# One core of a Perceiver block: stacked keys for the scores, two of three down blocks of the experts in split passes, and a new order in two passages

## The chip, the cores and the metric

The kernel is one program on one core of a Trainium2 chip. The metric is the time of one execution in device microseconds (us). Before the change it is 1679.32 us, the median of 3 runs (1677.81 to 1680.35).

## The reference, cut to what matters

A stream `x` of 512 rows (8 batches of 64 latents, width 512) passes six residual blocks in float32: causal cross attention to the first 64 context rows, self attention with tied queries and keys, a mixture of experts, masked cross attention to all 1601 context rows, causal self attention, and an int8 product. The change touches the third and the fourth, and the passage into each.

```python
# mixture of experts: 512 tokens, 64 experts, 8 per token; I = 352; two shared halves of the same size
rw = _route(x, gate_w, gate_bias)                       # [512, 64], 8 non-zero weights in a row
expert_out = silu(x @ Wg[e].T) * (x @ Wu[e].T) @ Wd[e].T
out = sum_e rw[:, e] * expert_out[e] + shared(x)        # shared = _mlp(x, Sg, Su, Sd)

# cross attention: 16 heads of 32, 8 batches, 64 queries, 1601 keys
attn = softmax(where(mask, -inf, einsum('bhqd,bhkd->bhqk', Q, K) * scale))
out = einsum('bhqk,bhkd->bhqd', attn, V) @ Wo + bo
```

## The kernel before, in words

Every engine has its own instruction list, written out by hand; semaphores join them. Nothing reorders an engine's list, so its order is the order of calls in the functions named here. PS is the PSUM, 8 banks of 512 floats.

**Float32 products in two ways.** A float32 matmul costs TensorE (PE) several internal passes; the trace counts two instructions for each. The large products are split instead: an operand is rounded to fp32r (`_hi`), the rest is `_lo`, and three fp32r passes hi*hi + hi*lo + lo*hi take its place (`gate_up` line 2144, `group` line 1267). ScalarE (ACT) makes the hi part by a copy, VectorE (DVE) the lo part by a subtraction; for the context GpSimd (POOL) makes the lo part.

**Shared experts and routing** (line 739 on). Per half tile k of 8: gate and up matmuls (`shared_in`), ACT's silu, DVE's product, three transposes of it, two ACT copies of these (`shared_ht`), and three float32 matmuls with the down weights (`shared_out`, which holds the transposes too, so PE waits between its two halves for the copies). Between them stand the matmuls of the routing tables (`table`), for which DVE works at the same time.

**Expert loop** (line 2130 on). 64 tiles of 128 token slots, four buffers k; tile i = 4r + k. On PE a step of tile i is: gate of i (12 matmuls), transposes of the hidden rows of i-1 (`hidden_t`), transposes of the gathered rows of i+1 (`rows_t`), up of i (12), down of i-1 (`down`: blocks of 128, 128 and 96 hidden rows, float32). ACT: silu, `rows_high`, `weights_high` of tile i+2, the weighted output `rows_out_copy`, and the issue of the two down-weight loads. DVE: `hidden_copy`, `rows_low`, `mul`, `weights_low`. SyncE (SP) loads the gate and up weights, POOL gathers the rows of a tile and scatters its output with add into HBM, each after a small copy of the slot numbers (lines 2085, 2100).

**Passage into the cross attention** (lines 1386 and 1576 on). PE makes 2 of the first batch's key chunks and 12 value tiles (`PRE[0]`), while the expert sums come back from HBM and are normalised; then it turns the rows (`xt_pe`), makes all four query blocks (`q_pe`), and the first scores with what is left of keys and value tiles (`PRE[1]`).

**Cross attention** (SEQ, line 1159). 32 units (batch b, dc); a unit handles four heads, and its list interleaves `k` (key chunk, 12 matmuls), `v` (value tile, 12), `s` (scores of a chunk), `T` (transposes of the probabilities of this unit), `P` (probabilities times values), `z` (divisors). The scores made in a unit are those of the next one. A chunk of keys (384, 384, 384 and 450 wide) has 128 feature rows: rows 0-63 belong to head pair p = 0, rows 64-127 to p = 1. `score` (line 1311) multiplies each half with the same half of the queries, 64 rows deep, three passes for each p, six matmuls in all. ACT writes a chunk's hi part (`key_high`), DVE its lo part (`key_low`), POOL the two parts of the queries (`take_q`).

## Time and profile before

| | |
|---|---|
| median of 3 runs | 1679.32 us |
| profiled execution | 1682.47 us, span 1680.6 us, mean granted TensorE clock 0.993 |
| front, first two attentions | 0 to 130 us |
| shared experts and routing | 130 to 214 us |
| expert loop | 214 to 679 us |
| passage into the cross attention | 679 to 740 us |
| cross attention, 8 batches | 740 to 1558 us |
| last attention and int8 block | 1558 to 1680.6 us |
| PE busy, over the span | 1634.1 us (97%) |
| DVE, ACT, POOL busy | 58%, 38%, 27% |

The bounds of the stages are read off the chain that ended last. In that chain PE holds 93% of the span. Its largest lines are L1305 (values, 18%), L1296 (keys, 17%), L2157 (gate and up, 14%), L2180 (down, 9%), L1323 (scores, 6%) and L1343 (transposes, 6%).

### The profile page before, as it was taken

To read this page: it belongs to the slowest core of one execution; us is meant where nothing else is said; L and a number is where in the kernel's file an instruction comes from. 1 tells how busy PE (TensorE), PEld (TensorE's weight loads), DVE (VectorE), ACT (ScalarE), POOL (GpSimd) and SP (SyncE) were. 2 spreads that over 40 slices of the span, in tenths; PEclk is the share of its full clock that TensorE was granted. 3 is DMA by queue.
4 is the path that set the end of the run, shared out by engine and by line. 5 is a ranking of instruction groups with operands and counts; after the bars stand their busy time and mean duration, and the time that the engine had idled before them with its cause. 6 is when DMAs were issued, how large, how long until landed. Compare 5 with 4: busy or idle time off the path is not lost.

```text
span 1680.6 us, 35189 instructions
## 1 busy us (share of the span) xinstructions
PE 1634.1 (97%) x13780; PEld 1351.0 (80%) x13781; DVE 966.9 (58%) x2076; ACT 637.0 (38%) x845; POOL 446.1 (27%) x453
## 2 busy tenths in 40 slices
PE   8999999999999999899999999999999999999897
PEld 5666677788777887778998989989899899898583
DVE  3877566667766666545444445454444544544666
ACT  1232156555655555223334233342242332423112
POOL 3110245555555554210302103021030210400100
PEclk9999999999999999999999999999999999999998
DMA  8003399999999998201102001020020200201200
GB/s 302 13 3 118 136 343 335 344 334 337 336 341 336 340 328 286 92 1 40 41 6 80 6 18 64 7 80 6 1 80 6 67 19 2 79 2 35 98 26 27
DMA packets 68476, 214.92 MB, mean 128 GB/s; under 512 B 13106, under 2 KB 30770, under 8 KB 58496
## 3 DMA queue, kind: packets, MB, share of 16 engines
q1 hardware_dynamic: 38656, 153.03, 25.3%
q10 hardware_dynamic: 15360, 43.26, 7.5%
q0 software_dynamic: 14336, 16.83, 4.8%
q8 instruction: 95, 1.56, 0.4%
q14 instruction: 29, 0.24, 0.0%
HBM read 208.07 MB, written 21.76 MB: 137 GB/s over the span
## 4 chain that ended last, share of the span: by engine, by line
PE 93%; DVE 2%; ACT 1%; DMA 1%; issue 1%; SPq 0%; POOL 0%; DVEq 0%; POOLq 0%; ACTq 0%
PE PS L1305 18%; PE PS L1296 17%; PE PS L2157 14%; PE PS L2180 9%; PE PS L1323 6%; PE PS L1343 6%; PE PS L1362 3%; PE PS L390 3%; PE PS L448 2%; PE PS L746 2%; PE PS L2141 2%; PE PS L411 1%; PE PS L762 1%; PE PS L2169 1%; PE PS L1698 1%
## 5 line engine op out<-in xcount | busy, mean ns | idle before, releaser
L1305 PE MATMUL PS<-S_r 128*128 128x256 f32 x2496 | 329.3, 286 | 1.9 <-DVE kh0l L1478 1.9
L1305 PEld LDWEIGHTS PS<-S_r 128*128 128x128 f32 x2496 | 305.0, 189 | 26.6 <-issue 22.2
L1296 PE MATMUL PS<-S_r 128*128 128x384 f32 (+1 forms) x1536 | 307.3, 349 | 0.0
L2157 PE MATMUL PS<-S_r,R_r 128*128 128x352 f32 x1152 | 298.8, 350 | 1.7 <-DVE R_r L2296 1.7
L1296 PEld LDWEIGHTS PS<-S_r 128*128 128x128 f32 x1536 | 266.2, 188 | 10.7 <-DVE kh0l L1478 2.0
L2157 PEld LDWEIGHTS PS<-S_r,R_r 128*128 128x128 f32 x1152 | 199.6, 189 | 20.5 <-issue 18.6
L1431 ACT COPY S<-PS 128x512 f32<-128x512 f32 (+1 forms) x128 | 64.4, 503 | 276.9 <-PE PS L1343 276.9
L1236 POOL COPY S<-qbd 128x128 f32<-128x128 f32 x32 | 9.4, 293 | 536.6 <-PE PS L1323 525.2
L1489 DVE CUSTOM_DVE_ANT_0 R<-PS,maskadd 128x384 f32<-128x384 f32 (+1 forms) x256 | 136.1, 569 | 17.9 <-PE PS L1323 17.9
L1471 DVE TENSOR_TENSOR R<-PS,vbias 128x256 f32<-128x256 f32 (+1 forms) x208 | 88.1, 424 | 101.3 <-PE PS L1305 96.6
L1219 POOL TENSOR_TENSOR S_r<-S,S_r 128x1536 fp32r<-128x1536 f32 (+2 forms) x31 | 114.0, 3686 | 119.7 <-ACT S_r L1408 119.6
L1425 ACT ACTIVATE R<-R,nmx 128x1601 f32<-128x1601 f32 x64 | 104.0, 1629 | 82.9 <-DVE nmx L1497 82.9
L2180 PE MATMUL PS<-R 128*128 128x512 f32 (+1 forms) x288 | 131.7, 593 | 1.3 <-DVE R L2306 1.3
L1478 DVE SCALAR_TENSOR_TENSOR kh0l<-PS,bias_c,kh0h 128x384 fp32r<-128x384 f32 x64 | 39.5, 618 | 141.6 <-ACT kh0h L1415 141.6
L2104 POOL DMA_INDIRECT moe_acc<-x,scol x64 | 102.4, 1600 | 57.1 <-PE PS L2141 36.1
L2019 DVE TENSOR_TENSOR R_r<-R,S_r 128x1408 fp32r<-128x1408 f32 x64 | 101.1, 1622 | 27.0 <-ACT S_r L2011 27.0
L1343 PE MATMUL PS<-ident,R 128*128 128x128 f32 (+1 forms) x832 | 114.1, 275 | 0.8 <-ACT R L1425 0.8
L1478 DVE SCALAR_TENSOR_TENSOR kh1l<-PS,bias_c,kh1h 128x384 fp32r<-128x384 f32 x64 | 41.7, 651 | 115.1 <-ACT kh1h L1415 115.1
L1523 DVE COPY S<-PS 128x512 f32<-128x512 f32 (+1 forms) x128 | 75.0, 586 | 53.8 <-PE PS L1343 53.4
L1343 PEld LDWEIGHTS PS<-ident,R 128*128 128x128 f32 (+1 forms) x832 | 93.7, 140 | 8.2 <-issue 3.0
L2011 ACT CAST S_r<-R 128x1408 fp32r<-128x1408 f32 x64 | 84.3, 1365 | 41.7 <-PE PS L2157 41.7
L2100 POOL COPY scol<-idx_tab 128x1 int32 (+1 forms) x64 | 62.2, 971 | 111.9 <-ACT x L2238 109.1
(261 smaller groups left out, 2462.6 us busy)
## 6 DMA issues: line engine op xcount, KB each, us to landing
R<-in_w_gu SPq DMA_DIRECT2D x34, 1408.0 KB, 9.7
R<-in_w_dna ACTq DMA_DIRECT2D x45, 512.0 KB, 5.5
qbd<-in_w_gu SPq DMA_DIRECT2D x16, 1408.0 KB, 9.4
S<-in_w_gu SPq DMA_DIRECT2D x16, 1408.0 KB, 9.5
S<-in_ctxT SPq DMA_DIRECT2D x24, 768.0 KB, 4.7
...
```

The lines of the kernel that those rows point to most:

```text
L1219: nc.gpsimd.tensor_tensor(lo, raw, hi.bitcast(F32), ALU.subtract).then_inc(s, 1)
L1296: last = nc.tensor.matmul(PS[:, bank, 0:n], w3[0][:, cc, f0:f0 + P], x3[i][:, cc, 0:n], start=(cc == 0 and w3 is wkv_hi and x3 is ctx_hi), ...
L1305: last = nc.tensor.matmul(PS[:, bank, 0:256], x3[need][:, cc, k0:k0 + P], w3[1][:, cc, f0:f0 + 256], start=(cc == 0 and w3 is wkv_hi and x ...
L1323: last = nc.tensor.matmul(PS[:, p, 0:n], q3[r:r + 64, :], k3[r:r + 64, 0:n], start=(q3 is qh and k3 is kh_), stop=(q3 is ql))
L1343: last = nc.tensor.transpose(PS[0:n, 2 + p, i * P:(i + 1) * P], sx[2 * (dc % 2) + p][:, kt * P:kt * P + n], ident[:, :])
L1425: nc.scalar.activation(v, v, ACT.Exp, scale=SC, bias=nmx[:, p:p + 1], accum_out=rsx[:, p:p + 1]).then_inc(px_ready, 1)
L1471: nc.vector.tensor_tensor(vx[hf][0:n, i, :], PS[0:n, bank_of(b, dc, ("v", i)), 0:256], vbias[0:n, hf * 256:hf * 256 + 256], ALU.add).then_ ...
L1489: nc.vector.tensor_tensor_reduce(out=sx[2 * ((dc + 1) % 2) + p][:, k0:k0 + n], in0=PS[:, p, 0:n], in1=maskadd[:, k0:k0 + n], scale=1.0, sc ...
L2019: nc.vector.tensor_tensor(wgu_lo[k][:, c, :, :], wgu[k][:, c, :, :], wgu_hi[k % 2][:, c, :, :].bitcast(F32), ALU.subtract).then_inc(wl_rea ...
L2104: pool.indirect_dma_start(out=acc[k % 2], out_offset=bass.IndirectOffsetOnAxis(ap=scol[:, k:k + 1], axis=0), in_=yrow[k], in_offset=None, ...
L2157: last = nc.tensor.matmul(PS[:, gu, 0:I], x3[:, c, :], w3[:, c, gu, :], start=(c == 0 and x3 is hi[0] and w3 is hi[1]), stop=(c == NC - 1 ...
L2180: last = nc.tensor.matmul(PS[:, 3, :], hT[0:w, j, :], wdn[k][0:w, j, :], start=(j == 0), stop=(j == 2))
```

## The change

The program does these things differently:

- **Scores.** For each p the keys are stacked: hi part in the 64 rows of p, lo part in the other 64. The queries of p stand twice, in both halves, once as hi and once as lo part. Two matmuls over all 128 rows per p, four a chunk, give (hi + lo)(hi + lo). `key_high`, `key_low` run once per p on 64 rows, DVE's output going to the other 64; `take_q` makes four small copies and two operations of twice the width.
- **Down blocks.** Blocks 0 and 1 of `down` become three fp32r passes each (`hT_hi`, `hT_lo`, `wdn_hi`, `wdn_lo`), block 2 stays float32 and comes first. ACT makes `hT_hi`, copies block 2 and makes `wdn_hi`; DVE makes `hT_lo` and `wdn_lo`.
- **Loads.** The down weights are loaded by SP behind the gate and up weights, no longer by ACT.
- **Slot numbers.** DVE copies a tile's two columns (`columns`); POOL's two small copies go.
- **Shared experts.** `shared_in` is called for gate and up apart, and the transposes are a piece of their own (`shared_turned`); the pieces are spread, and the last `shared_out` stands behind `rows_t(0, 0)`.
- **Passage.** `PRE` and DVE's list are reordered: `v0` ahead of `k0`, the four masks later, the query blocks among the first scores.

The diff, cut to its core (line indents are shortened):

```diff
...
-qraw, qzero = (R1[:, 2 * NC * SP + i * P:2 * NC * SP + (i + 1) * P] for i in range(2))
-kh = [[sb(f"kh{i}{half}", [P, KN[3]], F32R) for half in "hl"] for i in range(2)]
-qb = [[sb(f"qb{i}{half}", [P, P], F32R) for half in "hl"] for i in range(2)]
+qraw, qzero = (R1[:, 2 * NC * SP + 2 * i * P:2 * NC * SP + 2 * (i + 1) * P].rearrange("p (a m) -> p a m", a=2)
+               for i in range(2))
+kq = sb("kq", [P, 4 * KN[3] + 8 * P], F32R)
+keys = [[kq[:, (2 * i + p) * KN[3]:(2 * i + p + 1) * KN[3]] for p in range(2)] for i in range(2)]
+qb = [[kq[:, 4 * KN[3] + (4 * i + 2 * half) * P:4 * KN[3] + (4 * i + 2 * half + 2) * P]
+       .rearrange("p (a m) -> p a m", a=2) for half in range(2)] for i in range(2)]
+m = Arena(kq[:, :])
+wdn_hi = [m.view(2, D) for _ in range(2)]
+hT_lo = m.view(2, P)
...
+    def shared_turned(k):
+        hf = k % 2
         pe.wait_ge(sh_h, k + 1)
         if k >= 1:
             pe.wait_ge(sh_ht, k)
...
+    def shared_out(k):
+        t, hf = k // 2, k % 2
         pe.wait_ge(sh_ht, k + 1)
...
-PRE = ["k0 v0 v1 v2 k1 v3 v4 v5 v6 v7 v8 v9 v10 v11", "s0 k2 s1 k3 v12 s2 s3"]
+PRE = ["v0 k0 v1 v2 k1 v3 v4 v5 v6 v7 v8 v9 v10 v11", "q0 q1 s0 q2 k2 s1 k3 s2 v12 s3 q3"]
...
-        nc.gpsimd.tensor_copy(qraw[:, :].unsqueeze(1) if not isinstance(bv, int) else qraw[:, :],
-                              qbd[:, dc, bv, :]).then_inc(q_taken, 1)
-        pool.wait_ge(q_taken, 4 * b + dc + 1)
-        nc.gpsimd.tensor_tensor(hi[:, :], qraw[:, :], qzero[:, :], ALU.add).then_inc(qh_set, 1)
+        for i in range(4):
+            p, half = i // 2, i % 2
+            nc.gpsimd.tensor_copy(qraw[64 * half:64 * half + 64, p, :],
+                                  qbd[64 * p:64 * p + 64, dc, bv, :]).then_inc(q_taken, 1)
+            pool.wait_ge(q_taken, 4 * (4 * b + dc) + i + 1)
+        nc.gpsimd.tensor_tensor(hi[:, :, :], qraw[:, :, :], qzero[:, :, :], ALU.add).then_inc(qh_set, 1)
         pool.wait_ge(qh_set, 4 * b + dc + 1)
-        nc.gpsimd.tensor_tensor(lo[:, :], qraw[:, :], hi[:, :].bitcast(F32),
+        nc.gpsimd.tensor_tensor(lo[:, :, :], qraw[:, :, :], hi[:, :, :].bitcast(F32),
                                 ALU.subtract).then_inc(ql_ready, 1)
...
-        pe.wait_ge(kl_ready, 4 * h + c + 1)
-        if not (isinstance(b, int) and b < 0 and c == 0):
-            pe.wait_ge(sx_read, 8 * h + 2 * c)
-        (qh, ql), (kh_, kl_) = qb[(dc + 1) % 2], kh[c % 2]
-        for q3, k3 in ((qh, kh_), (qh, kl_), (ql, kh_)):
-            for p in range(2):
-                r = 64 * p
-                last = nc.tensor.matmul(PS[:, p, 0:n], q3[r:r + 64, :], k3[r:r + 64, 0:n],
-                                        start=(q3 is qh and k3 is kh_), stop=(q3 is ql))
-                if q3 is ql:
-                    last.then_inc(sx_made, 1)
+        for p in range(2):
+            pe.wait_ge(kl_ready, 8 * h + 2 * c + p + 1)
+            if h or c:
+                pe.wait_ge(sx_read, 8 * h + 2 * c + p - 1)
+            for half in range(2):
+                last = nc.tensor.matmul(PS[:, p, 0:n], qb[(dc + 1) % 2][half][:, p, :], keys[c % 2][p][:, 0:n],
+                                        start=(half == 0), stop=(half == 1))
+            last.then_inc(sx_made, 1)
...
-        nc.scalar.activation(kh[c % 2][0][:, 0:n], PS[:, bank_of(b, dc, ("k", c)), 0:n], ACT.Identity,
-                             bias=bias_c[:, 3, f:f + 1]).then_inc(kh_ready, 1)
+        for p in range(2):
+            r = slice(64 * p, 64 * p + 64)
+            nc.scalar.activation(keys[c % 2][p][r, 0:n], PS[r, bank_of(b, dc, ("k", c)), 0:n], ACT.Identity,
+                                 bias=bias_c[r, 3, f:f + 1]).then_inc(kh_ready, 1)
...
-        hi, lo = kh[c % 2]
-        dve.wait_ge(kh_ready, 4 * key_half(b, dc) + c + 1)
-        nc.vector.scalar_tensor_tensor(out=lo[:, 0:n], in0=PS[:, bank_of(b, dc, ("k", c)), 0:n],
-                                       scalar=bias_c[:, 3, f:f + 1], in1=hi[:, 0:n].bitcast(F32),
-                                       op0=ALU.add, op1=ALU.subtract).then_inc(kl_ready, 1)
+        for p in range(2):
+            r, other = slice(64 * p, 64 * p + 64), slice(64 - 64 * p, 128 - 64 * p)
+            k = keys[c % 2][p]
+            dve.wait_ge(kh_ready, 8 * key_half(b, dc) + 2 * c + p + 1)
+            nc.vector.scalar_tensor_tensor(out=k[other, 0:n], in0=PS[r, bank_of(b, dc, ("k", c)), 0:n],
+                                           scalar=bias_c[r, 3, f:f + 1], in1=k[r, 0:n].bitcast(F32),
+                                           op0=ALU.add, op1=ALU.subtract).then_inc(kl_ready, 1)
...
-    made(("k", 0), ("v", 0), ("v", 1))
+    made(("v", 0))
     first_rest(2, 0)
+    made(("k", 0), ("v", 1))
...
-    made(("v", 4))
-    set_mask(0, 0)
-    set_mask(0, 1)
-    made(("v", 5))
-    set_mask(0, 2)
-    set_mask(0, 3)
-    made(("v", 6))
...
-    made(("v", 10))
     for t in range(NT):
         last = nc.vector.bn_aggr(mv[:, t, :], st[:, t, :])
     link(last)
     nc.vector.tensor_scalar(rstd[:, :], mv[:, :, 1], EPS, None, ALU.add).then_inc(mv_ready, 1)
+    made(("v", 10))
+    set_mask(0, 0)
     dve.wait_ge(rstd_ready, MV[3] + 1)
     scaled(0)
...
-    q_dve(dve, 2, 2, bank=2)
+    set_mask(0, 1)
+    set_mask(0, 2)
+    set_mask(0, 3)
     for w in PRE[1]:
...
+        def load_dn(r, k):
+            i = NBUF * r + k
+            ev = expert(r, k)
+            if not (isinstance(r, int) and r == 0):
+                sp.wait_ge(y_made, i - NBUF + 1)
...
-        with sp.Fori(1, n) as r:
+        for k in range(NBUF):
+            load_gu(1, k)
+            if k:
+                load_dn(1, k - 1)
+        with sp.Fori(2, n) as r:
             for k in range(NBUF):
-                load(r, k)
+                load_gu(r, k)
+                load_dn(*tile_before(r, k))
+        load_dn(n - 1, NBUF - 1)
...
-            pool.wait_ge(tables, 1)
+            col_set, turned = (count(pool, v) for v in (i + 1, i - NBUF + 1))
             pool.wait_ge(rows_out, 32)
             if not (isinstance(r, int) and r == 0):
-                pool.wait_ge(xg_made, i - NBUF + 1)
-            nc.gpsimd.tensor_copy(gcol[:, k:k + 1], idx_tab[:, column(r, k)]).then_inc(gcol_set, 1)
-            col_set = count(pool, i + 1)
-            pool.wait_ge(tables, 1)
-            pool.wait_ge(gcol_set, col_set)
+                pool.wait_ge(xg_made, turned)
+            pool.wait_ge(cols_set, col_set)
...
+        for i in range(2):
+            rest(wkv_lo[i], slot[1 + 2 * i], wkv_hi[i], w_lo, w_hi, i + 1)
         n = iterations(pool)
         for k in range(NBUF):
             gather(0, k)
...
-            for j, (i0, w) in enumerate(IJ):
-                last = nc.tensor.matmul(PS[:, 3, :], hT[0:w, j, :], wdn[k][0:w, j, :],
-                                        start=(j == 0), stop=(j == 2))
+            nc.tensor.matmul(PS[:, 3, :], hT[0:IJ[2][1], 2, :], wdn[k][0:IJ[2][1], 2, :], start=True, stop=False)
+            pe.wait_ge(dl_ready, i + 1)
+            for j in range(2):
+                for h3, w3 in ((hT_hi, wdn_hi[k % 2]), (hT_lo, wdn_hi[k % 2]), (hT_hi, wdn_lo[k])):
+                    last = nc.tensor.matmul(PS[:, 3, :], h3[:, j, :], w3[:, j, :],
+                                            start=False, stop=(j == 1 and w3 is wdn_lo[k]))
             last.then_inc(y_made, 1)
...
         rows_t(0, 0)
+        shared_out(2 * NT - 1)
...
-        def load_down(r, k):
-            e = act.value_load(eot_row[0:1, column(r, k)], min_val=0, max_val=E - 1)
...
+        def hidden_high(r, k):
+            i = NBUF * r + k
+            act.wait_ge(ht_made, i + 1)
+            if not (isinstance(i, int) and i == 0):
+                act.wait_ge(y_made, i)
+            nc.scalar.copy(hT[0:96, 2, :], PS[0:96, 2, 2 * P:3 * P])
+            nc.scalar.copy(hT_hi, PS[:, 2, 0:2 * P].rearrange("p (a b) -> p a b", a=2)).then_inc(hh_ready, 1)
+        def down_high(r, k):
+            i = NBUF * r + k
+            act.wait_ge(w_dn[k], 32 * (r + 1))
+            if not (isinstance(r, int) and r == 0 and k < 2):
+                act.wait_ge(y_made, i - 1)
+            nc.scalar.copy(wdn_hi[k % 2], wdn[k][:, 0:2, :]).then_inc(dh_ready, 1)
...
+            if not (isinstance(r, int) and r == 0 and k == 0):
+                hidden_high(*tile_before(r, k))
             if not (final and k == NBUF - 1):
                 rows_high(*tile_after(r, k))
+            down_high(r, k)
             if not (final and k >= NBUF - 2):
                 weights_high(*tile_after(*tile_after(r, k)))
             if not (isinstance(r, int) and r == 0 and k == 0):
                 rows_out_copy(*tile_before(r, k))
-                if not (final and k):
-                    load_down(*(tile_before(r + 1, k) if k else (r, NBUF - 1)))
...
+        hidden_high(n - 1, NBUF - 2)
+        down_high(n - 1, NBUF - 1)
         act.wait_ge(u_made, NBUF * n - 1)
         ctx_high(0, 0)
         act.wait_ge(u_made, NBUF * n)
         ctx_high(0, 1)
+        hidden_high(n - 1, NBUF - 1)
...
-        def hidden_copy(r, k):
+        def hidden_low(r, k):
             i = NBUF * r + k
-            dve.wait_ge(ht_made, i + 1)
+            dve.wait_ge(hh_ready, i + 1)
             if not (isinstance(i, int) and i == 0):
                 dve.wait_ge(y_made, i)
-            nc.vector.tensor_copy(hT[:, 0:2, :], PS[:, 2, 0:2 * P].rearrange("p (a b) -> p a b", a=2))
-            nc.vector.tensor_copy(hT[0:96, 2, :], PS[0:96, 2, 2 * P:3 * P]).then_inc(ht_ready, 1)
-        first_dve(dve)
+            nc.vector.tensor_tensor(hT_lo, PS[:, 2, 0:2 * P].rearrange("p (a b) -> p a b", a=2),
+                                    hT_hi.bitcast(F32), ALU.subtract).then_inc(ht_ready, 1)
+        def down_low(r, k):
+            dve.wait_ge(dh_ready, NBUF * r + k + 1)
+            nc.vector.tensor_tensor(wdn_lo[k], wdn[k][:, 0:2, :], wdn_hi[k % 2].bitcast(F32),
+                                    ALU.subtract).then_inc(dl_ready, 1)
...
+        def columns(r, k, final):
+            dve.wait_ge(xg_loaded[k], 16 * r)
...
+                last = nc.vector.tensor_copy(cols[:, k, :], pairs[:, k, at])
+            last.then_inc(cols_set, 1)
...
+            columns(r + 1, k, final)
             mul(r, k)
+            down_low(r, k)
             if not (final and k >= NBUF - 2):
                 weights_low(*tile_after(*tile_after(r, k)))
...
```

The three places of which the prediction speaks. First PE in the shared experts. `R,xnT` are gate or up matmuls, `ident,R` the transposes of the hidden rows, `R 128x512` the down matmuls, `S` those of the routing. Before:

```order
L746 MATMUL PS<-R,xnT 128x352 x16
L756 MATMUL PS<-ident,R 128x128 x2
L756 MATMUL PS<-ident,R 96x128
L762 MATMUL PS<-R 128x512 x3
L746 MATMUL PS<-R,xnT 128x352 x8
L756 MATMUL PS<-ident,R 128x128 x2
L756 MATMUL PS<-ident,R 96x128
L762 MATMUL PS<-R 128x512 x3
L784 MATMUL PS<-S 128x64 x10
L787 MATMUL PS<-S 128x64 x4
L746 MATMUL PS<-R,xnT 128x352 x8
```

After:

```order
L753 MATMUL PS<-R,xnT 128x352 x16
L763 MATMUL PS<-ident,R 128x128 x2
L763 MATMUL PS<-ident,R 96x128
L753 MATMUL PS<-R,xnT 128x352 x4
L772 MATMUL PS<-R 128x512 x3
L753 MATMUL PS<-R,xnT 128x352 x4
L763 MATMUL PS<-ident,R 128x128 x2
L763 MATMUL PS<-ident,R 96x128
L798 MATMUL PS<-S 128x64 x10
L801 MATMUL PS<-S 128x64 x4
L772 MATMUL PS<-R 128x512 x3
L753 MATMUL PS<-R,xnT 128x352 x8
```

Between a half tile's transposes and its down matmuls there now stand four matmuls of another, or routing.

Second ACT in the expert loop, one tile: `R<-PS 128x352` is the silu, `R_r<-PS 128x512` `rows_high`, the two 1408-wide casts `weights_high`, `x<-PS,w_tab` the weighted output. Before:

```order
L2227 ACTIVATE R<-PS 128x352 [waits h_ready,g_made]
L2220 CAST R_r<-PS 128x512 [waits u_made,xg_made]
L2011 CAST S_r<-qbd 128x1408 [waits u_made,w_gu0]
L2011 CAST S_r<-qbd 128x1408
L2238 ACTIVATE x<-PS,w_tab 128x512 [waits y_made]
L2242 TENSOR_LOAD eot_row
L2242 ISA x2
L2244 ISA
L2244 DMA xnT<-in_w_dna 128x1024
L2246 ISA
L2246 DMA xnT<-in_w_dnb 96x512
```

After:

```order
L2278 ACTIVATE R<-PS 128x352 [waits h_ready,g_made]
L2297 COPY R<-PS 96x128 [waits y_made,ht_made]
L2298 CAST R_r<-PS 128x256
L2268 REGISTER_ALU
L2271 CAST R_r<-PS 128x512 [waits u_made,xg_made]
L2306 CAST kq<-xnT 128x1024 [waits y_made,w_dn1]
L2049 CAST S_r<-R 128x1408 [waits u_made,w_gu3]
L2049 CAST S_r<-R 128x1408
L2288 ISA [waits y_made]
L2289 ISA [waits y_added0]
L2289 ACTIVATE x<-PS,w_tab 128x512
```

The three copies of the hidden rows and of the down weights (`kq`) are new, and the loads are gone.

Third PE at the start of the cross attention. `kh..,qb..` (before) and `kq` (after) are scores, `xnT,R` query blocks, `S_r 128x384` and `128x450` key chunks, `S_r 128x256` value tiles. Before:

```order
L348 MATMUL PS<-ident,S 128x128 x16
L369 MATMUL PS<-xnT,R 128x512 x16
L1323 MATMUL PS<-kh0h,qb0h 128x384 x2
L1323 MATMUL PS<-kh0l,qb0h 128x384 x2
L1323 MATMUL PS<-kh0h,qb0l 128x384 x2
L1296 MATMUL PS<-S_r 128x384 x12
L1323 MATMUL PS<-kh1h,qb0h 128x384 x2
L1323 MATMUL PS<-kh1l,qb0h 128x384 x2
L1323 MATMUL PS<-kh1h,qb0l 128x384 x2
L1296 MATMUL PS<-S_r 128x450 x12
L1305 MATMUL PS<-S_r 128x256 x12
```

After:

```order
L359 MATMUL PS<-ident,S 128x128 x16
L379 MATMUL PS<-xnT,R 128x512 x8
L1355 MATMUL PS<-kq 128x384 x4
L379 MATMUL PS<-xnT,R 128x512 x4
L1330 MATMUL PS<-S_r 128x384 x12
L1355 MATMUL PS<-kq 128x384 x4
L1330 MATMUL PS<-S_r 128x450 x12
L1355 MATMUL PS<-kq 128x384 x4
L1339 MATMUL PS<-S_r 128x256 x12
L1355 MATMUL PS<-kq 128x450 x4
L379 MATMUL PS<-xnT,R 128x512 x4
L1339 MATMUL PS<-S_r 128x256 x12
```

Six half-deep matmuls a chunk (three rows of two) become four full ones, and the query blocks stand apart.

## Rows read from the trace of the kernel before

**Rows 1.** Windows: us; busy us (instructions) of each engine; clock; DMA share; GB/s.

```profile
430.00:437.20 7.20, 7.20 (x39) 5.74 (x39) 5.05 (x7) 4.43 (x6) 3.85 (x4) 1.00 1.01 334
900.00:1007.20 107.20, 106.97 (x1131) 96.68 (x1130) 51.79 (x159) 36.07 (x53) 19.29 (x16) 1.00 0.11 34
```

**Rows 2.** Chain that ended last, expert loop: start us, us, what.

```profile
657.07 1.92 PE PS L2157 x12
658.99 2.58 PE PS L2180 x6
...
666.20 2.58 PE PS L2180 x6
```

**Rows 3.** Groups by line and form: busy us, mean ns, idle before.

```profile
L2011 ACT CAST S_r<-R 128x1408 fp32r<-128x1408 f32 x64 | 84.3, 1365 | 41.7 <-PE PS L2157 41.7
...
L2227 ACT ACTIVATE R<-PS 128x352 f32<-128x352 f32 x64 | 29.7, 464 | 80.8 <-PE PS L2157 74.0 <-issue 6.9
```

**Rows 4.** Timeline of DVE and ACT, routing: start us, us, instruction.

```profile
139.78 0.37 ACT L813 COPY R<-PS 128x256 f32<-128x256 f32 x1 [2.23 <-PE PS L756]
140.05 0.26 ACT L814 COPY R<-PS 96x128 f32<-96x128 f32 x1
...
169.65 1.22 DVE L1119 TENSOR_TENSOR S<-S 128x1024 f32<-128x1024 f32 x1
```

**Rows 5.** Windows of the first loads, as Rows 1.

```profile
2.00:4.00 2.00, 0.00 (x0) 0.00 (x0) 0.00 (x0) 0.00 (x0) 1.26 (x10) 1.00 0.94 299
...
10.00:12.00 2.00, 2.00 (x6) 0.82 (x5) 0.00 (x0) 0.00 (x0) 0.00 (x0) 1.00 1.04 431
```

**Rows 6.** Timeline of the expert loop: a gather and its wait.

```profile
501.10 2.24 POOL L2089 DMA_INDIRECT S<-moe_rows,gcol  x1 [0.83 <-POOL gcol L2085]
...
512.38 0.66 PE L2141 MATMUL PS<-ident,S 128*128 128x128 f32 x4 [1.07 <-DMA S<-moe_rows,gcol]
```

**Rows 7.** Chain that ended last, cross attention.

```profile
812.11 1.42 PE PS L1305 x12
...
814.40 2.09 PE PS L1296 x12
816.49 0.72 PE PS L1323 x6
817.21 3.04 PE PS L1305 x24
...
830.61 2.50 PE PS L1296 x12
...
838.50 0.81 PE PS L1323 x6
```

**Rows 8.** Timeline of PE's weight loads at a score.

```profile
742.48 0.19 PEld L1323 LDWEIGHTS PS<-kh0h,qb1h 64*128 64x128 f32 x2 [0.25 <-issue]
```

**Rows 9.** Timeline, first scores of a unit with dc = 2.

```profile
899.28 0.56 ACT L1415 ACTIVATE kh0h<-PS,bias_c 128x384 fp32r<-128x384 f32 x1
...
899.87 0.62 DVE L1478 SCALAR_TENSOR_TENSOR kh0l<-PS,bias_c,kh0h 128x384 fp32r<-128x384 f32 x1 [3.21 <-ACT kh0h L1415]
```

**Rows 10.** Chain that ended last, shared experts to first expert.

```profile
139.42 0.34 PE PS L756 x3
...
140.37 2.85 PE PS L762 x6
...
211.86 0.56 DVE x L1019
...
213.22 0.70 DVE R_r L2296
```

**Rows 11.** Timeline and chain, passage into the cross attention.

```profile
684.88 4.63 PE L1305 MATMUL PS<-S_r 128*128 128x256 f32 x24 [1.94 <-DVE kh0l L1478]
...
710.13 13.97 PE PS L369 x32
...
736.41 3.35 ACT R L1425 x4
```

More of the change, by code:

```diff
@@ L66, in perceiver @@
         x = sb("x", [P, NT, D])
-        xnT = sb("xnT", [P, NC, T])
+        with nc.sbuf_tensor("xnT", [P, NC, T], F32) as xnT:
+            pass
+        xnT_r = sb("xnT_r", [P, NC, T], F32R)
         with nc.sbuf_tensor("qbd", [P, NC, B, P], F32) as qbd:
@@ L737, in first_pe, with shared_in @@
             logits(3)
-            def shared_in(k):
+            def shared_in(k, gu):
                 t, hf = k // 2, k % 2
                 if k >= 2:
-                    pe.wait_ge(sh_silu, k - 1)
-                    pe.wait_ge(sh_h, k - 1)
-                for gu in range(2):
-                    for c in range(NC):
-                        last = nc.tensor.matmul(PS[:, 2 + 2 * hf + gu, 0:I], xnT[:, c, t * P:(t + 1) * P],
-                                                wgu[2 + hf][:, c, gu, :], start=(c == 0), stop=(c == NC - 1))
-                    last.then_inc(sh_u if gu else sh_g, 1)
-            def shared_out(k):
-                t, hf = k // 2, k % 2
+                    pe.wait_ge(sh_h if gu else sh_silu, k - 1)
+                for c in range(NC):
+                    last = nc.tensor.matmul(PS[:, 2 + 2 * hf + gu, 0:I], xnT[:, c, t * P:(t + 1) * P],
+                                            wgu[2 + hf][:, c, gu, :], start=(c == 0), stop=(c == NC - 1))
+                last.then_inc(sh_u if gu else sh_g, 1)
+            def shared_turned(k):
+                hf = k % 2
                 pe.wait_ge(sh_h, k + 1)
@@ L774, in first_pe @@
             pe.wait_ge(ld_sh, 96)
-            shared_in(0)
-            shared_in(1)
+            shared_in(0, 0)
+            shared_in(0, 1)
+            shared_in(1, 0)
+            shared_in(1, 1)
+            shared_turned(0)
+            shared_in(2, 0)
             shared_out(0)
-            shared_in(2)
-            shared_out(1)
+            shared_in(2, 1)
+            shared_turned(1)
             pe.wait_ge(sel_ready, 1)
@@ L2037, in load @@
                                  a["w_gu2"][ev, :, :].rearrange("e p n -> (e p) n")).then_inc(w_gu[k], 16)
-                    if not isinstance(r, int):
-                        return
-                    if k == 1:
+                def load_dn(r, k):
+                    i = NBUF * r + k
+                    ev = expert(r, k)
+                    if not (isinstance(r, int) and r == 0):
+                        sp.wait_ge(y_made, i - NBUF + 1)
+                    elif k == 1:
                         sp.wait_ge(sh_u, 2 * NT)
@@ L2051, in _ @@
                 for k in range(NBUF):
-                    load(0, k)
+                    load_gu(0, k)
+                    load_dn(0, k)
                     if k == NBUF - 1:
@@ L2112, in _ @@
                     gather(0, k)
-                for i in range(2):
-                    rest(wkv_lo[i], slot[1 + 2 * i], wkv_hi[i], w_lo, w_hi, i + 1)
                 for k in range(NBUF):
@@ L2194, in step @@
                         down(*before)
-                first_pe(pe)
+                shared_out = first_pe(pe)
                 n = iterations(pe)
@@ L2264, in _ @@
                 weights_high(0, 1)
-                for r in range(2):
-                    for k in range(NBUF):
-                        step(r, k)
-                with act.Fori(2, n - 1) as r:
+                for k in range(NBUF):
+                    step(0, k)
+                with act.Fori(1, n - 1) as r:
                     for k in range(NBUF):
```

128 lines of the change are left out of this document (76 added, 52 removed).

## The prediction, made before the changed kernel was run

> **What bounds the kernel now.** I read the page first: TensorE (PE) is busy 97% of the span and holds 93% of the chain that ended last. Then the windows, one expert tile and one batch of the cross attention [rows 1]: PE is busy 7.20 of 7.20 us and 106.97 of 107.20, the next engine (DVE) 5.05 and 51.79. The reader is to see that a saving counts only if it shortens PE's own list, and that ACT (4.43 and 36.07) and DVE have room for more work. Last the chain of waits at the two passages [rows 10, 11], where PE does stop. All sums are made in the profiled execution, 1682.5 us; the median of before is 3.2 us lower, and that is taken off at the end.
>
> **Down blocks, 64 tiles.** Six PE records of a tile's `down` take 2.58 us, 0.43 each [rows 2]. Four of them (blocks 0 and 1) become six fp32r passes of 512 columns. The trace has such passes at other widths: 256 wide 1.42/12 = 0.118, 384 wide 2.09/12 = 0.174, 450 wide 2.50/12 = 0.208 [rows 7], 352 wide 1.92/12 = 0.16 [rows 2]. The line through the first two gives 0.230 at 512. Bounds: 0.16, if width cost nothing, and 0.43, the float32 record. I take 0.23, since four widths lie near one line. So 4 x 0.43 = 1.72 becomes 6 x 0.23 = 1.38, 0.34 less; a tile goes from 7.20 to 6.86, and 64 tiles give 21.8 us. The ends would be +48 and -55.
>
> That holds only if nobody else needs more than 6.86. ACT: 4.43 [rows 1], the two copies of hidden rows 0.37 + 0.26 [rows 4], and the 1024-wide copy of weights, which is not in the trace: between 0.46 at 352 columns and 1.37 at 1408 [rows 3] the line gives 1.04. Sum 6.1. DVE: 5.05 + 1.22 for the 1024-wide subtraction, as the one in the routing [rows 4]; the hidden subtraction takes the place of the old copies; 6.3 at most. Both fit, with 0.5 to 0.8 us to spare. The copies stand ahead of work that PE wants soon: behind `hidden_high` on ACT is `rows_high`, needed by the next gate. Between the transposes and the passes PE has the gathered rows, up (1.92) and block 2 (0.86), which is their cover. Data: 334 GB/s over 7.20 us [rows 1] is 2.40 MB a tile; in 6.86 us that is 351 GB/s. The first loads show 431 for one stretch and 299 for another [rows 5].
>
> POOL loses two small copies before each gather and scatter. One gather kept PE waiting 1.07 us [rows 6]; that its margin grows could give back about 1 us, that the clock of the loads now rests on one queue could take as much. I count nothing.
>
> **End of the expert loop.** On ACT a 1.5 us context copy now stands ahead of the hidden copy of the last tile, and DVE and the last passes are queued behind that. Block 2 covers part of it. Cost 1.0; bounds 0 and 2.
>
> **Shared experts and routing.** From the transposes of a half tile at 139.42 to the end of its down matmuls at 140.37 + 2.85 = 143.22 are 3.80 us [rows 10]. Without the stop it is 0.34 + 2.58 = 2.92, so the stop costs 0.88: two copies, and matmuls that start slower behind it. The chain shows eight such stops; work of another half tile, or routing, now stands in each: 8 x 0.87 = 7.0. The last one is followed by the sum, then two wait steps, and the first expert's gate begins after 213.92 (first row of that stretch at 211.86) [rows 10], 2.1 us; `rows_t(0, 0)` now stands ahead of the last `shared_out`, so they lie beside it. New waits: where a table's matmuls move ahead PE reaches DVE's selection earlier, about 0.6, and the first two tiles' extra copies, 0.5. Sum 8.0; bounds 4 and 10. For the first tiles' loads, which now queue behind gate and up weights, and for a fuller PE in the first stretch I add 0.5, bounds -2 and +2.
>
> **Passage into the cross attention.** PE waits 1.94 us for the first keys' lo part [rows 11]; with `v0` (1.42) ahead of `k0`, 1.4 of it is covered. That alone would buy nothing, since PE waits again later, for DVE to normalise the rows. But DVE's sums start behind the sixth value tile that PE has made, so they come 1.4 earlier too, and one value copy of DVE (0.4) moves behind them: 1.8 in all, counted once. The masks leave a place where DVE waits for PE anyway, nothing. The query blocks took 13.97 in one piece, 3.49 each [rows 11]. Now the first score waits for POOL after two of them: four copies and two double-width operations, some 3 us, with one block (q1) as cover: 1.5 lost at most beyond what it costs now. At the end the fourth block and a value tile stand where PE waited 3.35 us for the exponentials [rows 11]; 3.1 of that goes. Sum 1.8 + 3.1 - 1.5 = 3.4; bounds 0 and 7.
>
> **Scores, 32 units.** A chunk of 384 takes 0.72 [rows 7]: 3 x 0.174 for three pairs of half-deep matmuls that run together, and 0.2 ahead of them. The timeline of weight loads shows the same idle piece, 0.25 at a score's start [rows 8]. Behind a chunk there is one more: 24 value matmuls take 3.04, where twice 1.42 is 2.84 [rows 7], 0.20. So a chunk costs 0.92. Between two full-depth kinds no such piece is in the chain (value tile 812.11 + 1.42, then transposes, then keys at 814.40). Four full matmuls: 4 x 0.174 = 0.70, 0.22 less; the 450-wide chunk 0.81 + 0.20 against 4 x 0.208 = 0.83, 0.18 less. Two p: a unit handles four chunks, 3 x 0.22 + 0.18 = 0.84, times 32 = 27. Of that I take off 0.5: at units with dc = 2 PE reaches the first score while ACT and DVE still write its keys [rows 9], and that takes one step of 0.6 more, eight times, mostly made up by the later ones. 26.5. Bounds: -24 (below) and +27. ACT and DVE get some 2.3 and 2.5 us a unit of 26.8; they have 17 and 13 idle.
>
> [...]
>
> **Sum.** 8.0 + 0.5 + 21.8 - 1.0 + 3.4 + 26.5 = 59.2; 1682.5 - 59.2 - 3.2 = 1620.1, say 1620.
>
> **Rivals.**
> - A, the loop does not get shorter: the data rate or the ACT chain holds the tile at 7.20. For: a mean rate of 334 GB/s of which 351 is asked, DMA share 1.00 or more already [rows 1], ACT only 0.7 us from full, and a gather that has already made PE wait [rows 6]. Against: 431 GB/s for a stretch [rows 5], and PE never idles for weights now. Then 21.8 is missing: 1642. Chance 0.17.
> - B, the 0.4 us around scores belong to something other than half depth, a wait or a change of source, and stay: a chunk takes 0.2 + 0.70 + 0.20 = 1.10, 0.18 more than now; 128 chunks lose 24 instead of gaining 26.5: 1620 + 50 = 1670. Against: [rows 8] name no releaser, only the engine's own issue, and no other neighbours show it. Chance 0.09.
> - C, slower than before: with all weights on one queue, each load behind the one before it, the rate falls to the 299 GB/s of the first stretch [rows 5] or less, since the down weights no longer overlap the gate and up weights. Every microsecond a tile costs 64. The other terms give 37.4, so the point is 7.20 + 37.4/64 = 7.78 us a tile, 309 GB/s; at 288 GB/s a tile takes 8.35 and the time is 1620 + 64 x 1.49 = 1715. Against: in [rows 5] the same single queue reached 431. Chance 0.05.
> - D, the change does not do what it says in the passages: the moved pieces expose as much as they hide, 8.0 + 3.4 go: 1631. Chance 0.08.
>
> **How the numbers follow.** The forecast has 0.58, with a range of its own from 1609 to 1632 (the terms' bounds, not all at one end). 0.03 is for less than that range: passes at 0.21 and a gather margin that gives back more. Between A and C nothing lies near 1679. A measurement of this kernel can tell 0.2%, 3.4 us, from no change. Faster: forecast, the better end, A, B and D, less what B and A together could undo (1692 at worst): 0.93. Same 0.02, slower 0.05. The range 1606 to 1648 holds the forecast, the better end nearly whole, D and A.
>
> **What would show it.** A tile's window of 6.86 with PE busy throughout: right; PE idle with a DMA or `dh_ready` behind it: A or C. Passes of 512 columns at 0.23. Scores at 0.70 a chunk with no issue gap on either side; a gap there is B. In the chain, no stops of ACT copies between 139 and 209, and no 3.35 at 736. Wrong would be a tile above 7.0, or chunks at 0.9 or more.

## The result and the profile after

The changed kernel takes 1661.23 us, the median of 4 runs (1658.25 to 1663.44); before, in the same session, 1679.84 (1677.81 to 1682.33). The ratio is 0.9887, 95% interval 0.9875 to 0.9899: 18.6 us less, where 59 were forecast, and outside the forecast range. The profiled execution has a span of 1658.2 us at a clock of 0.996.

First a window of the changed kernel over most of the expert loop, with columns as in [rows 1].

```profile
240.00:640.00 400.00, 387.38 (x2164) 338.12 (x2164) 320.59 (x389) 301.17 (x442) 194.58 (x112) 1.00 1.01 337
```

Then its window of one batch of the cross attention, which was 107.20 us long in [rows 1] and has PE full as before:

```profile
900.00:1005.80 105.80, 105.63 (x1101) 100.95 (x1104) 62.65 (x175) 46.22 (x68) 25.09 (x29) 1.00 0.11 34
```

The same stretch of the loop in the kernel before:

```profile
240.00:640.00 400.00, 398.93 (x2044) 316.78 (x2043) 276.18 (x332) 241.17 (x277) 217.26 (x222) 1.00 1.00 336
```

PE was full before (398.93 of 400); now it stands still for 12.6 us. What did not move is at the right: DMA share 1.00 and 1.01, 336 and 337 GB/s. The chain that ended last, from the page after, says the same: it goes through transfers for 9% of the span and through DVE for 6%, where it was 1% and 2% before.

```profile
PE 79%; DMA 9%; DVE 6%; issue 2%; ACT 2%; SPq 1%; POOL 0%; DVEq 0%; ACTq 0%; POOLq 0%
```

The waits of the changed kernel for weights in that stretch, and those behind them (engine and line, releaser: us in total, times, longest). POOL's waits for outputs to scatter are longer, but in this view no engine waits for POOL.

```profile
ACT S_r L2049 <- DMA R<-in_w_gu: 40.2, 24, 3.3
DVE R_r L2057 <- ACT S_r L2049: 32.3, 24, 3.0
...
ACT S_r L2049 <- DMA S<-in_w_gu: 24.1, 13, 3.2
ACT S_r L2049 <- DMA qbd<-in_w_gu: 23.8, 13, 3.7
...
PE PS L2226 <- DVE kq L2367: 11.9, 13, 2.0
```

ACT's `weights_high` (L2049) waits for gate and up weights, 88 us in 400; before, it waited for PE [rows 3]. DVE's low part of the weights (L2057) stands behind it. PE does not wait for the weights themselves but for the low part of the hidden rows (L2367), ahead of block 2: that part and ACT's `hidden_high`, from which it is made, stand in the lists of DVE and ACT behind the late weights.

Where PE has what it needs, a tile is what was forecast. Chain of the changed kernel, one early tile: six fp32r passes take 1.37 to 1.39 (1.36 to 1.41 over the loop), block 2 0.86, and the tile 6.87.

```profile
236.48 1.93 PE PS L2204 x12
238.41 0.33 PE PS L2216 x3
238.74 0.44 PE PS L2188 x4
239.18 1.93 PE PS L2204 x12
241.10 0.86 PE PS L2226 x2
241.96 1.39 PE PS L2230 x6
243.35 1.92 PE PS L2204 x12
```

Boundaries common to both traces give the account. They are the end of the first tile's down, the end of the last one's, and the moments at which SyncE issues a batch's context (790.24 and 778.66 us, and six batches later 1433.46 and 1413.51).

| stretch | before | after | gain | forecast |
|---|---|---|---|---|
| to the end of the first tile's down | 228.17 | 222.73 | 5.4 | 8.8 |
| the other 63 tiles | 451.29 | 448.69 | 2.6 | 20.5 |
| passage and two units | 110.78 | 107.24 | 3.5 | 5.1 |
| six batches (107.20 and 105.81 each) | 643.2 | 634.9 | 8.4 | 19.9 |
| the rest | 247.1 | 244.7 | 2.5 | 5.0 |
| span | 1680.6 | 1658.2 | 22.4 | 59.2 |

Not all of this gain is the change's; part is TensorE's clock in the two executions that were traced. In the trace before, PE stood still for 1.71 us ahead of the first expert's gate, and in the 4 us behind it the granted clock is 0.57. The trace of before_less_data (below), the same kernel up to there, has the same stop of 1.71 and then a clock of 1.00. Where the clock is 0.57 the gate's matmuls start 0.29 us apart (214.91 to 216.67), at 1.00 they start 0.16 apart. First before, then before_less_data:

```profile
214.00:218.00 4.00, 4.00 (x17) 3.93 (x17) 3.64 (x2) 1.94 (x3) 3.17 (x3) 0.57 0.97 367
214.00:218.00 4.00, 4.00 (x26) 3.71 (x25) 3.82 (x4) 1.88 (x4) 2.87 (x2) 1.00 0.97 382
```

From that gate to the end of the first tile's down they take 14.20 and 12.64 us. The trace before has a second such stretch in the passage (684 to 690 us, clock 0.72): passage and two units take 110.78 us there and 109.25 in before_less_data. So about 1.6 of the 5.4 and 1.5 of the 3.5 are the clock's. That leaves 3.8 where 8.8 were forecast and 2.0 where 5.1 were, and 19.3 in all, close to the 18.6 of the medians. Other executions of the changed kernel have such a stretch as well. In after_again (below) the same passage takes 110.2 us and not 107.24, with

```profile
699.00:706.00 7.00, 6.12 (x14) 3.20 (x15) 2.61 (x6) 0.59 (x1) 0.00 (x0) 0.51 0.09 32
```

where the trace after has a clock of 1.00. The stretch of 63 tiles scatters for another reason, its transfers: 448.7 to 451.5 us in five traces with the changed loop, 451.3 and 451.6 in two with the loop before. Of the 20.5 forecast for it, 0 to 3 came.

### The profile page after: what moved, and what is told of

Same layout as the page of the kernel before. It is cut to its first block, busy times and chain, and to the rows that moved or that the text cites. A ratio compares the mean times of both kernels' runs of the same rounds, so it can differ in the third digit from the quotient of the medians.

```text
span 1658.2 us, 35538 instructions
## 1 busy us (share of the span) xinstructions
PE 1604.1 (97%) x13652; PEld 1404.3 (85%) x13653; DVE 1112.2 (67%) x2269; ACT 790.0 (48%) x1164; POOL 464.7 (28%) x421
## 4 chain that ended last, share of the span: by engine, by line
PE 79%; DMA 9%; DVE 6%; issue 2%; ACT 2%; SPq 1%; POOL 0%; DVEq 0%; ACTq 0%; POOLq 0%
PE PS L1339 17%; PE PS L1330 17%; PE PS L2204 9%; DMA R<-in_w_gu 6%; PE PS L1374 6%; PE PS L1355 5%; PE PS L2230 3%; PE PS L1393 3%; PE PS L399 3%; PE PS L457 2%; PE PS L2226 2%; PE PS L420 1%; PE PS L753 1%; DMA qbd<-in_w_gu 1%; DMA S<-in_w_gu 1%
## 5 line engine op out<-in xcount | busy, mean ns | idle before, releaser
L1339 PEld LDWEIGHTS PS<-S_r 128*128 128x128 f32 x2496 | 312.1, 188 | 12.5 <-DVE kq L1515 7.6
L1515 DVE SCALAR_TENSOR_TENSOR kq<-PS,bias_c,kq 64x384 fp32r<-64x384 f32 (+1 forms) x256 | 162.3, 634 | 214.6 <-ACT kq L1450 209.9
L1330 PEld LDWEIGHTS PS<-S_r 128*128 128x128 f32 x1536 | 268.1, 188 | 6.4 <-issue 0.5
L2204 PE MATMUL PS<-S_r,R_r 128*128 128x352 f32 x1152 | 273.2, 328 | 0.2 <-DVE R_r L2358 0.2
L1450 ACT ACTIVATE kq<-PS,bias_c 64x384 fp32r<-64x384 f32 (+1 forms) x256 | 151.1, 590 | 209.4 <-PE PS L1330 205.8
L2151 POOL DMA_INDIRECT moe_acc<-x,cols x64 | 124.8, 1950 | 217.8 <-ACT x L2289 121.2
L1268 POOL COPY S<-qbd 64x128 f32<-64x128 f32 x128 | 36.9, 288 | 495.0 <-PE PS L1355 478.8
L2057 DVE TENSOR_TENSOR R_r<-R,S_r 128x1408 fp32r<-128x1408 f32 x64 | 101.1, 1622 | 34.3 <-ACT S_r L2049 34.3
L1355 PE MATMUL PS<-kq 128*128 128x384 f32 (+1 forms) x512 | 121.1, 355 | 2.1 <-POOL kq L1273 1.3
L2138 POOL DMA_INDIRECT S<-moe_rows,cols x64 | 96.5, 1508 | 68.3 <-DVE cols L1162 32.6
L2049 ACT CAST S_r<-R 128x1408 fp32r<-128x1408 f32 x64 | 84.5, 1367 | 47.6 <-DMA R<-in_w_gu 43.1
```

What stands on the lines that cost most here:

```text
L1330: last = nc.tensor.matmul(PS[:, bank, 0:n], w3[0][:, cc, f0:f0 + P], x3[i][:, cc, 0:n], start=(cc == 0 and w3 is wkv_hi and x3 is ctx_hi), ...
L1339: last = nc.tensor.matmul(PS[:, bank, 0:256], x3[need][:, cc, k0:k0 + P], w3[1][:, cc, f0:f0 + 256], start=(cc == 0 and w3 is wkv_hi and x ...
L1355: last = nc.tensor.matmul(PS[:, p, 0:n], qb[(dc + 1) % 2][half][:, p, :], keys[c % 2][p][:, 0:n], start=(half == 0), stop=(half == 1))
L1450: nc.scalar.activation(keys[c % 2][p][r, 0:n], PS[r, bank_of(b, dc, ("k", c)), 0:n], ACT.Identity, bias=bias_c[r, 3, f:f + 1]).then_inc(kh ...
L1515: nc.vector.scalar_tensor_tensor(out=k[other, 0:n], in0=PS[r, bank_of(b, dc, ("k", c)), 0:n], scalar=bias_c[r, 3, f:f + 1], in1=k[r, 0:n]. ...
L2057: nc.vector.tensor_tensor(wgu_lo[k][:, c, :, :], wgu[k][:, c, :, :], wgu_hi[k % 2][:, c, :, :].bitcast(F32), ALU.subtract).then_inc(wl_rea ...
```

## The experiments

Ratios are to the kernel before, run on the same chip. The changed kernel was run a second time, unaltered, as a yardstick:

> The changed kernel once more, unaltered, beside orders_act on the same chip, as a measure of the scatter of the loop: 1661 within 3, a rate of 335 to 339 GB/s between 240 and 640 us.

1660.66 us, 0.9883 (0.9864 to 0.9901), 337 GB/s. Two sessions agree within 0.6 us.

**The loop: less data.**

```diff
-                    sp.dma_start(wdn[k][0:96, 2, :], a["w_dnb"][ev, :, :]...).then_inc(w_dn[k], 16)
+                    if isinstance(r, int) and r == 0:
+                        sp.dma_start(wdn[k][0:96, 2, :], a["w_dnb"][ev, :, :]...).then_inc(w_dn[k], 16)
...
-                    pe.wait_ge(w_dn[k], 32 * (r + 1))
+                    pe.wait_ge(w_dn[k], 16 * (r + 2))
...
-                    act.wait_ge(w_dn[k], 32 * (r + 1))
+                    act.wait_ge(w_dn[k], 16 * (r + 2))
```

> The changed kernel, but the third down block (96 rows, 192 KB) is loaded only for the first four tiles; later tiles reuse it, so the product of the experts is not the reference's. Theory D (the rate of all DMA engines together holds the tile at about 7.17 us: 2.40 MB at 335 GB/s): 2.20 MB take 6.57 us, less than PE's 6.86, so the loop becomes PE bound and shortens by 0.3 x 63 = 19 us, to about 1642. Rival E (the copies of ACT and DVE hold the tile): nothing of theirs is removed, no change, 1661 within 2.

1639.94 us, 0.9761 (0.974 to 0.9782): 21 less than the changed kernel. The same window of the loop in less_data:

```profile
240.00:640.00 400.00, 400.00 (x2272) 355.50 (x2270) 343.97 (x409) 322.56 (x465) 183.00 (x116) 1.00 0.95 324
```

And the group of `weights_high` on its page (busy, mean ns, idle before and its releaser):

```profile
L2049 ACT CAST S_r<-R 128x1408 fp32r<-128x1408 f32 x64 | 84.5, 1369 | 13.2 <-PE PS L2205 12.6
```

PE is full, the DMA share has fallen below 1, and ACT waits for PE again. In the changed kernel's page that group reads

```profile
L2049 ACT CAST S_r<-R 128x1408 fp32r<-128x1408 f32 x64 | 84.5, 1367 | 47.6 <-DMA R<-in_w_gu 43.1
```

ACT and DVE do more in these 400 us than in the changed kernel and hold nobody up: theory E falls. The other 63 tiles take 429.9 us, 21.4 less than before the change, where 20.5 were forecast.

**The loop: more PE work.**

```diff
                     for h3, w3 in (...):
-                            last = nc.tensor.matmul(..., start=False, stop=(j == 1 and w3 is wdn_lo[k]))
+                            last = nc.tensor.matmul(..., start=False, stop=False)
+                    last = nc.tensor.matmul(PS[:, 3, :], hT_lo[:, 1, :], wdn_lo[k][:, 1, :], start=False, stop=True)
```

> The changed kernel with one more fp32r pass (lo times lo of block 1) in each down product, 0.23 us of PE a tile. Theory D: PE's tile goes from 6.86 to 7.09, still under the 7.17 that the transfers need, so the time stays at 1661 within 3. Rival P (PE is still the bound of the loop and lost the gain in small stops): 64 x 0.23 = 14.7 more, 1676. Rival E (ACT and DVE chain): between the two.

1661.38 us, 0.9888 (0.9864 to 0.9911): no change, where a loop bound by PE would have taken 14.7 us more. In 400 us of the loop PE is busy 394.78 rather than 387.38; the pass went into time in which PE stood still. In this trace the 63 tiles take 452.2 us, just above the scatter given above, so up to 2 us of the passes may show.

```profile
240.00:640.00 400.00, 394.78 (x2212) 347.27 (x2211) 323.52 (x387) 305.20 (x445) 180.65 (x111) 1.00 1.01 336
```

**The kernel before with less data** (the same edit to its loads).

> The kernel before, with the third down block loaded only for the first four tiles (as in less_data; the product is not the reference's). Theory D: in the kernel before PE (7.20 us a tile) and the transfers (2.40 MB at 337 GB/s, 7.13) were both full; with 8% less data PE still needs 7.20, no change, 1680 within 3. Rival (transfers were the bound before as well): 10 us or more less.

1680.61 us, ratio 1.0002 (0.9988 to 1.0017). Before, transfers were full but hid behind PE.

```profile
240.00:640.00 400.00, 400.00 (x2063) 319.66 (x2062) 277.84 (x335) 241.84 (x279) 217.77 (x222) 1.00 0.92 311
```

**Down weights on a second queue.**

```diff
                 for k in range(NBUF):
                     load_gu(1, k)
-                    if k:
-                        load_dn(1, k - 1)
                 with sp.Fori(2, n) as r:
                     for k in range(NBUF):
                         load_gu(r, k)
-                        load_dn(*tile_before(r, k))
-                load_dn(n - 1, NBUF - 1)
...
                             rows_out_copy(*tile_before(r, k))
+                        if not (final and k):
+                            load_down(*(tile_before(r + 1, k) if k else (r, NBUF - 1)))
```

> The changed kernel with the down weights of the loop issued by ACT on its own queue again, as in the kernel before. Theory D (the sum of all transfers is the bound, whichever queue carries them): 1661 within 4. Rival C (one queue for all weights costs rate): the loop comes down toward PE's 6.86 us a tile, 1645 or less.

1654.09 us, 0.9852 (0.9829 to 0.9875): 7 less. Neither expectation holds whole. The share is still 1.01, so the loop is still bound by transfers, but it moves 343 GB/s, and the 63 tiles take 443.4 us. The edit changes two things at once: the queue, and the moment of issue (behind ACT's `rows_out_copy`, no longer behind SP's load of gate and up weights).

```profile
240.00:640.00 400.00, 391.35 (x2193) 342.58 (x2192) 332.46 (x396) 311.65 (x450) 178.72 (x114) 1.00 1.01 343
```

**Routing: pieces of PE's list moved.**

```diff
             shared_turned(1)
+            shared_in(3, 0)
             pe.wait_ge(sel_ready, 1)
...
             shared_out(1)
-            shared_in(3, 0)
             shared_in(3, 1)
...
+            shared_in(4, 1)
             pe.wait_ge(eot_ready, 1)
             nc.tensor.transpose(PS[0:2, 0, 0:P], eot[:, :], ident[:, :]).then_inc(eot_made, 1)
-            shared_in(4, 1)
...
             shared_in(5, 1)
+            shared_in(6, 0)
             table(0)
             shared_turned(4)
+            shared_in(6, 1)
             table(1)
...
-            shared_in(6, 0)
-            shared_in(6, 1)
```

The changed kernel, PE's waits from 139 to 200 us:

```profile
PE PS L779 <- DVE S L1152: 3.1, 3, 1.7
PE PS L798 <- DVE S L1089: 0.4, 1, 0.4
PE PS L812 <- DVE eot L1117: 0.4, 1, 0.4
```

> The changed kernel with pieces of PE's list moved in the shared experts and routing: a gate or up piece ahead of each place where PE waits for a table of DVE (shared_in(3, 0) ahead of the ranks, shared_in(4, 1) ahead of the tile numbers, shared_in(6, 0) and (6, 1) ahead of table(0) and table(1)). Theory R (PE stood still 3.9 us there because DVE's chain of tables sets their time, and the pieces that could have filled it stood behind): 3.5 to 4 us less, 1657. Rival (DVE's chain sets the end of the stage whatever PE does, since the first gather waits for the tables): no change or 1 us slower.

1655.51 us, 0.9859 (0.9837 to 0.9882): 5.7 less. Of that 3.4 is in this stage: the second tile's gate starts at 211.75, after 215.15 in the changed kernel.

```profile
177.02 2.87 PE L779 MATMUL PS<-S 128*128 128x192 f32 x16 [0.59 <-DVE S L1152]
...
211.75 2.19 PE L2204 MATMUL PS<-S_r,R_r 128*128 128x352 f32 x12 [0.16 <-DVE R_r L2358]
```

One wait of 0.59 is left of 3.9. The loop, bound by its transfers, ends 2.5 us earlier (668.93, before that 671.42), and the span is 4.4 shorter. Of this, 1.6 fell in the last stretch of the table, where the changed kernel's trace has two stretches of lowered clock (0.59 from 1538 to 1542 us, 0.72 from 1568 to 1574) and that of pe_order has none before 1646. Without it 2.8 are left. Why the medians show 5.7 isn't settled; both kernels' runs spread over 5 us and more.

**Cross attention: the small transposes moved.**

```diff
-        SEQ = ["... k3 s2 v3 v4 T3 s3 v5 v6 P2 P3",
-               "... k3 s2 v10 v11 T3 s3 P2 P3",
+        SEQ = ["... k3 s2 v3 T3 v4 s3 v5 v6 P2 P3",
+               "... k3 s2 v10 T3 v11 s3 P2 P3",
...
-               "... k3 s2 v8 v9 v10 T3 s3 v11 v12 P2 P3"]
+               "... k3 s2 v8 T3 v9 v10 s3 v11 v12 P2 P3"]
```

The timeline of the changed kernel behind a last key chunk:

```profile
924.09 2.70 PE L1330 MATMUL PS<-S_r 128*128 128x450 f32 x12
...
926.62 0.87 PE L1355 MATMUL PS<-kq 128*128 128x384 f32 x4
926.82 1.29 ACT L1450 ACTIVATE kq<-PS,bias_c 64x450 fp32r<-64x450 f32 x2 [2.53 <-PE PS L1330]
927.33 4.79 PE L1339 MATMUL PS<-S_r 128*128 128x256 f32 x36
927.56 1.40 DVE L1515 SCALAR_TENSOR_TENSOR kq<-PS,bias_c,kq 64x450 fp32r<-64x450 f32 x2 [2.45 <-ACT kq L1450]
```

ACT and DVE empty the bank at 928.96. The score and one value tile (0.70 + 1.42) bring PE to 928.75, and the next tile, for the same bank, waits. Between 846 and 1376 us the view of waits has this 15 times:

```profile
PEld PS L1339 <- DVE kq L1515: 4.0, 15, 0.3
PEld PS L1355 <- DVE kq L1515: 1.6, 5, 0.3
```

> The changed kernel with the order of units dc = 0, 1 and 3 of the cross attention changed: the two transposes T3 stand between v3 and v4 (v10 and v11, v8 and v9), no longer behind the last of them. Theory B (the second value tile behind a key chunk waits for the bank that ACT and DVE empty in four steps, 2.35 us after the chunk, and PE has only 2.1 us of work until then): the 0.22 of T3 fills most of the 0.26 stop, 3 x 0.22 x 8 = 5 us less, 1656. Rival (the stop is small or comes back at the next piece): within 1 us of 1661.

1658.66 us, 0.9871 (0.9849 to 0.9893). The first of the two rows above is gone and the second is the same. A batch takes 105.10 instead of 105.81 in the traces, 0.7 x 8 = 5.6. The median shows 2.6 of it; in this trace the loop, which the edit doesn't touch, ended at 674.22 and not at 671.42, and the passage has 4 us at a clock of 0.57. The gain in time is therefore not clear of the scatter by itself; the batch in the trace is, and both_orders (below) has it again.

**Scores of full depth, in the kernel before.**

```diff
-                for p in range(2):
-                    r = 64 * p
-                    last = nc.tensor.matmul(PS[:, p, 0:n], q3[r:r + 64, :], k3[r:r + 64, 0:n], ...)
+                last = nc.tensor.matmul(PS[:, 0, 0:n], q3[:, :], k3[:, 0:n], ...)
...
```

> The kernel before; each score chunk is three full-depth matmuls of 128 rows instead of six of 64 rows (three pairs). The scores of the two head pairs are then summed in one bank and the other bank is stale, so the output is not the reference's; the time of three matmuls is that of three pairs. Theory S (the 0.20 us ahead of and behind a score belong to half depth): a chunk falls from 0.92 to 0.52, 128 x 0.40 = 51 less, 1629. Rival B (they belong to a wait or to the change of operands): no change, 1680.

1637.67 us, 0.9753 (0.9734 to 0.9772): 42 less, not 51. A batch falls from 107.20 to 101.77, that is 5.43 / 16 = 0.34 a chunk. The stops belong to half depth, as theory S has it, but cost 0.06 less together than I had read off [rows 7].

**Both orders, and with the second queue.**

> pe_order and t3_earlier in one kernel. Theory: the two act in different stages and add up: 4 less (routing) and 5 less (cross attention) than the changed kernel in the trace's stages; 1652, with about 3 us of scatter from the loop's transfers. Rival (what is won in the routing is lost again in the loop, since the transfers set its end): 1656.

1652.81 us, 0.9842 (0.9826 to 0.9859). A batch takes 105.08, the second gate starts at about 211.5; the two add up.

> both_orders with the down weights of the loop issued by ACT again (as in loads_from_act). If the second queue is worth what loads_from_act showed (343 against 337 GB/s in the loop, 6 us), 1646 to 1647. If that was scatter between chips or runs, 1652 as both_orders.

1644.79 us, 0.9794 (0.9776 to 0.9811): 8.0 less than both_orders, and 16 less than the changed kernel. It beats both kernels.

```profile
240.00:640.00 400.00, 393.97 (x2223) 347.23 (x2222) 337.59 (x400) 315.79 (x457) 178.19 (x113) 1.00 1.01 347
```

The rate of the second queue is there a second time (347 against 337), and was no scatter. Of 400 us PE still stands still for 6: the transfers are still the bound. The 63 tiles take 440.2 us.

## Why the prediction was wrong, point by point

- **Which resource was full.** The step that failed first is "What bounds the kernel now": engines were compared with PE, the transfers were not. [Rows 1] had DMA share 1.01 at 334 GB/s: sixteen engines busy all the time, and 351 GB/s was asked of them. In no run did the loop, from 240 to 640 us, get above a share of 1.01; the most it moved was 347. The 431 GB/s of [rows 5] was taken as proof of room, but it came from another mix of transfers, with no gathers or scatters beside it, and it too had a share of 1.04. The forecast read the rate and not the share. So rival A was true for the loop, in its data half: with 8% less data the gain appears (less_data), with more PE work nothing is lost (one_more_pass), and before the change less data bought nothing (before_less_data). The term for the down blocks was 20.5 in the account; 2.6 came in the two traces, 0 to 3 over all. A had a chance of 0.17; the row that settled it was cited under it.
- **A second cause on the same resource.** Moving the down loads to SyncE, behind the gate and up weights, was counted as "nothing". It costs 7 to 8 us (loads_from_act, orders_act), because in a stage bound by transfers 2% of rate is 2% of time. Rival C had the direction and too large a size: 337 GB/s, never 299. The two causes divide what was missing: the 63 tiles take about 450 us with one queue, 440 to 443 with two, and 430 with less data.
- **Down passes.** Right: 1.38 forecast, 1.36 to 1.41 measured; the tile 6.87 where weights are there.
- **Shared experts and routing.** Of 8.0 less than 4 came: the first expert's gate starts at 210.14 instead of 213.97. The stops of `shared_out` went, as forecast (7.0; the view of waits has 5.0 for them, 8 of 0.62, and 0.2 after; the rest lies in the matmuls behind each, six in 2.85 us [rows 10] where the tiles' six take 2.58 [rows 2]). What was late next was DVE's chain of tables: PE waits for it in five places, 3.9 us, where the sum had 0.6 and 0.5 for all new waits. PE's own stops had covered DVE's chain, and taking them away brought PE to the tables earlier than DVE. pe_order gave 3.4 of it back.
- **Scores.** The mechanism was right (B falls: 0.70 and 0.83 a chunk, and before_full_depth), its size was not. Half depth costs 0.34 a chunk, not 0.40: 12 x (0.34 - 0.174) + 4 x (0.34 - 0.208) = 2.5 a batch instead of 3.36. Then two waits, of which the sum had only the second, at 0.5 us for all batches. The bank of a key chunk is emptied in four steps instead of two, 0.7 a batch (t3_earlier), and the first score of dc = 2 waits for its keys:

```profile
887.44 0.98 PE PS L1355 x4
```

  0.98 against 0.70 once a batch. 2.5 - 0.7 - 0.28 = 1.5; measured 107.20 - 105.81 = 1.4. The last part was read off the trace and not tried.
- **Half depth against full depth.** The second and third half-deep pair of a chunk start 0.17 apart (816.70 and 816.87 us in the trace before), the time of one full matmul (0.174, [rows 7]), and their stretch costs 0.34 on the way in and out together (before_full_depth), against 0.174 for the fourth full matmul. The way in and out weighed more.
- **Passages.** Too large. With the clock's part taken off, passage and two units gave 2.0 where 5.1 were forecast. The view of waits has 7.2 us of PE's stops between the loop and 740 us before and 6.1 after, 1.1 less where the passage had 3.4; the two units gave about 0.7. The new stop for POOL is 1.34 (1.5 forecast):

```profile
708.22 0.97 PE L1355 MATMUL PS<-kq 128*128 128x384 f32 x4 [1.34 <-POOL kq L1273]
```

  The step that failed here is the end of the passage. The 3.35 us that [rows 11] gives ACT's exponentials was read as a wait of PE, but a piece of the chain is the time of the engine that is in it, and PE worked beside it. Its stop was 0.82, so 3.1 could not go. The kernel before:

```profile
736.27 2.28 PE L1296 MATMUL PS<-S_r 128*128 128x384 f32 x12
...
739.80 0.66 PE L1343 MATMUL PS<-ident,R 128*128 128x128 f32 x4 [0.82 <-ACT R L1425]
```

  At its start the stop of 1.94 for the first keys became two, of 0.65 and 0.55, and PE reaches the turning of the rows 0.8 earlier behind the loop (25.1 us; 25.9 in before_less_data, whose clock is full there), where 1.8 was forecast. So rival D was right in part: of the 11.4 us that it put in doubt, about 5 came.

What stays open: why two queues move more than one when all sixteen engines are busy either way, whether the gain is the queue's or that of the moment of issue, and how much of the rate the gathers and scatters take; none of these was tried apart. Nor is it shown why the clock falls behind a stop of PE in one execution and not in another.
